# A decoder layer with routed experts on one core: the first normalisation goes to ScalarE, u and k_lo move forward in their lists

## The chip, the cores and the metric

The kernel runs on 1 core of one Trainium2 chip. The metric is the device time of one execution in microseconds, the median of several runs.

## The reference

Input x is 32 sequences of 256 tokens with 256 channels, all float32. Three sublayers follow one another, each with a residual and a layer normalisation:

```python
x = layernorm(x + attn(x))           # a complex decay over the first axis: real(conv) * x
x = layernorm(x + xattn(x, ctx))     # 16 heads of 16 channels, relu projections, softmax, own layernorm
x = layernorm(x + ffn(x))            # rms norm, nearest of 8 centroids picks the expert, a * silu(g)
```

The first sublayer is a recurrence over the 32 items: a complex state per (token, channel) is multiplied by a fixed complex decay and the item is added; the real part (+1 for the residual) times x is what is called u below, and its normalisation over the channels is x1. The cross attention takes queries from x1 and keys and values from the context of the same item.

## The kernel before, in words

There are two phases. Phase 1 makes the first two sublayers and writes each token's row into a bucket of its expert in HBM. Phase 2 runs the experts over tiles of 128 rows; the change does not touch it.

Phase 1 is a software pipeline over the items, unrolled: each engine has its own list, written out by hand, and steps t from -2 to 34 call the same `step(t)` on it. Semaphores alone tie the lists together; an engine never passes an instruction of its own list that waits. In step t the engines work on several items at once: `cur` = t (scores for the maxima), `prv` = t-1 (transposed scores and exponentials), `n` = t+1 (projections), `nn` = t+2 (u and x1), `a` = t-2 (output of the attention and its normalisations), `b` = t-3 (choice of the expert, scatter). Inside a step TensorE, ScalarE and VectorE go through h = 0 to 15; at every even h they do a pair of heads (h, h+1) and, behind it, the other work that the code hangs on that h.

What the change and the prediction speak of:

- TensorE. `scores` (L693) needs the stacks of q and k, which are read from HBM in two halves of 8 heads (`stack_in`), and the maximum of the head two before, because the PSUM banks of the scores are used in turn. `transposed_scores` (L706) needs the exponential of two heads before. The first score matmul of a step is called S0. Then come the flip of x1 (L649 at h = 0, into M_ps[0], which needs `x1_ok` and `ctT_ok`), Q's projection (h = 2, 3), K's projection (L677 at h = 6, 7; it needs the first division of item a, `o_ok`), V's (h = 11, 12).
- VectorE. `maxima` (L888) for a pair of heads takes two instructions. At h = 0 the second normalisation into `row` (L901, waits for `rstd2`). At h = 3 u (L909), one instruction over 128x512 with two inputs in SBUF, `state` and `xt`; at h = 4 its statistics, at h = 5 its moments, between the two parts of `divide`. At h = 11 `slots` and `gain`, at h = 12 y2 (L967, waits for `rstdx`), at h = 13 the two instructions of x1 (L973), which wait for `rstd1` and `y_ok`. L1032 is a small instruction of `pick` with two inputs in SBUF.
- GpSimd. Its list of a step is: `conv_products` (L407, by_re), `weigh` (L465), the bias onto x1 (L495), `cut` for q, `offset`, `conv_real`, `rstd` for ln1, `conv_imag(0)` (L423), `cut` for k (L483, makes k_lo = k32 - k_hi), `conv_imag(1)` (L426), `rstd` for lnx, the two scatters (L513, which wait for the slots from VectorE), `conv_input` (L433, the last of the conv's five counts), `rstd` for ln2 and `rms`.
- ScalarE. Exponentials (L559), the copies of q (L595) and of k (L603: k_hi twice, then k32 twice, by channel half), v_aug (L612) at h = 13, qn at h = 14 and ctT (L580) at h = 15, each behind the pair of that h or of the one before.
- SP, the queue of DMA issues. For item n in order: q pieces out, `read_q` of the first half, k_hi out, wait for `k_cut`, k_lo out (L288), the row of the maxima out (L276), `read_k` of the first half (L301, L302, which waits until both pieces of k are in HBM), and the rest.

Two excerpts, GpSimd's place and the place of x1 on VectorE:

```python
conv_imag(t + 3, 0)
cut(n, k32[:, :, :], k_hi, k_lo, "k_ok", "k_cut", k_out)
conv_imag(t + 3, 1)
```

```python
if h == 13 and active(nn):
    wait(dve, "rstd1", nn, 2)
    wait(dve, "y_ok", nn - 4, 4)
    for c in range(NTC):
        v.tensor_scalar(x1[:, nn.mod(4), c], u[:, c], mv1[:, c, 0:1], rs1[:, 1, c:c + 1],
                        ALU.subtract, ALU.mult).then_inc(s["x1_ok"], 1)
```

Of the kernel before, what the change touches and what calls it, by code (L numbers as in the profile page):

```python
# [10 lines left out]
ALU = mybir.AluOpType  # L11
# [3 lines left out]
P = 128  # L15
# [62 lines left out]
def build(nc, x, ctx_in, lmlg, theta, last_conv, Wq, bq, Wk, bk, Wv, bv, ln_g, ln_b, ffn_scale, centroids, up_w, down_w, out):  # L78
    stack = ExitStack()
    with stack:  # L80
# [33 lines left out]
        def sb1(name, shape, dt=F32):  # L114
            return phase1.enter_context(nc.sbuf_tensor(name, shape, dt))

        with phase1:
# [23 lines left out]
            st1 = sb1("st1", [P, NTC, 6])  # L141
            mv1 = sb1("mv1", [P, NTC, 2])
            rs1 = sb1("rs1", [P, 2, NTC])
            x1 = sb1("x1", [P, 4, NTC, C])
            x1T = sb1("x1T", [P, NCH, TOK])
            ctT = sb1("ctT", [P, NCH, TOK])
# [53 lines left out]
                x_in0 x_in1 ctx_in0 ctx_in1 conv u_ok ln1 rstd1 x1_ok x1T_pe x1T_ok ctT_pe ctT_ok  # L200
                q_pe q_ok k_pe k_ok q_cut k_cut v_pe v_ok q_out0 q_out1 k_out0 k_out1 stack0 stack1 s_pe max_ok
                negT neg_ok neg_out neg_in0 neg_in1 t_pe exp_ok pv o_ev x_pe o_ok qn_pe qn_ok oq_ok lnx rstdx
                x1b_ok y_ok ln2 rstd2 x2_ok rms xw_ok offset nx_ok xnT_pe xnT_ok dist_pe pick rank_pe slot_ok
                id_ok scat0 scat1 pool_waits sp_waits dve_waits"""
            s = {n: sem(n) for n in names.split()}
            x_in, ctx_in_s, q_out, k_out, stack_in = ([s[a + "0"], s[a + "1"]] for a in ("x_in", "ctx_in", "q_out", "k_out", "stack"))
# [161 lines left out]
            def _(pool):  # L368
# [116 lines left out]
                def step(t):  # L485
                    n, a, b = t + 1, t - 2, t - 3
                    first = t.k < 0
                    if first:
                        rstd(t + 2, "ln1", 4, mv1, rs1, "rstd1")
                    conv_products(t + 3)  # L490
                    weigh(b)
                    if active(a):
                        wait(pool, "x1_ok", a, 2)
                        wait(pool, "x1T_pe", a)
                        g.tensor_tensor(x1[:, a.mod(4)], x1[:, a.mod(4)], b_bc[:, :].unsqueeze(1).to_broadcast([P, NTC, C]),  # L495
                                        ALU.add).then_inc(s["x1b_ok"], 1)
                    cut(n, q32[:, :, :], q_hi, q_lo, "q_ok", "q_cut", q_out)
                    offset(b)
                    conv_real(t + 3)
                    if not first:  # L500
                        rstd(t + 2, "ln1", 4, mv1, rs1, "rstd1")
                    conv_imag(t + 3, 0)
                    cut(n, k32[:, :, :], k_hi, k_lo, "k_ok", "k_cut", k_out)
                    conv_imag(t + 3, 1)
                    rstd(a, "lnx", 4, mvx, rsx, "rstdx")
                    if active(b):

                        p = b.mod(2)
                        wait(pool, "slot_ok", b, SLOT)
                        wait(pool, "id_ok", b)  # L510
                        wait(pool, "rms", b, 4)
                        for c in range(NTC):
                            g.indirect_dma_start(out=buckets[:, :], out_offset=bass.IndirectOffsetOnAxis(ap=slot[:, p, c:c + 1], axis=0),  # L513
                                                 in_=row[:, p, c, :], in_offset=None, bounds_check=PAD - 1,
                                                 oob_is_err=False).then_inc(scat[p], 16)
                    conv_input(t + 3)
                    rstd(a, "ln2", 4, mv2, rs2, "rstd2")
                    rms(a)
# [9 lines left out]
            def _(act):  # L528
# [33 lines left out]
                def step(t):  # L562
                    prv, n, a, b = t - 1, t + 1, t - 2, t - 3
                    for h in range(H):
# [44 lines left out]
                        if h == 13 and active(n):  # L609
                            wait(act, "v_pe", n, 2)  # L610
                            wait(act, "pv", n - 4, 4)
                            a_.activation(v_aug[:, n.mod(4), :, 0:H * VW].rearrange("p k (h w) -> p k h w", w=VW)[:, :, :, 0:DH],  # L612
                                          M_ps[1][:, :].rearrange("p (k h w) -> p k h w", k=NTC, w=DH), ACT.Relu).then_inc(s["v_ok"], 1)
                        if h == 4 and active(b):

                            wait(act, "xw_ok", b)
                            wait(act, "rms", b, 4)
                            wait(act, "offset", b - 1)
                            for c in range(NTC):
                                if c:  # L620
                                    wait(act, "nx_ok", b, 2, 1)
                                a_.activation(junk[:, :], xw[:, c], ACT.Square, scale=row[:, b.mod(2), c, C:C + 1],
                                              accum_out=nx[:, c:c + 1]).then_inc(s["nx_ok"], 1)
# [201 lines left out]
            def _(dve):  # L825
# [65 lines left out]
                def step(t):  # L891
                    cur, prv, nn, a, b = t, t - 1, t + 2, t - 2, t - 3
                    for h in range(H):
                        if h % 2 == 0:
                            maxima(cur, h)
                            maxima(cur, h + 1)
                        if h == 0 and active(b):
                            wait(dve, "rstd2", b, 2)
                            wait_ring(dve, scat[b.mod(2)], b - 2, 2, 16 * NTC)
# [1 line left out]
                                v.tensor_scalar(row[:, b.mod(2), c, 0:C], y2[:, c], mv2[:, c, 0:1], rs2[:, 1, c:c + 1],  # L901
                                                ALU.subtract, ALU.mult).then_inc(s["x2_ok"], 1)
                            v.tensor_copy(row[:, b.mod(2), :, C + 1].bitcast(I32), ids[:, b.k]).then_inc(s["id_ok"], 1)
                        if h == 3 and active(nn):

                            wait(dve, "x1_ok", nn - 1, 2)
                            wait(dve, "conv", nn, 5)
                            wait_ring(dve, x_in[nn.mod(2)], nn, 2, 16)
                            v.scalar_tensor_tensor(u[:, :, :], state[:, 0], 1.0, xt[:, nn.mod(2)], ALU.add, ALU.mult).then_inc(s["u_ok"], 1)  # L909
                        if h == 4 and active(nn):  # L910
                            wait(dve, "u_ok", nn)
                            wait(dve, "rstd1", nn - 1, 2)
                            stats(nn, u, st1, "ln1")
                        if h == 5:
                            if active(a):
                                divide(a, 0, 0)
                            if active(nn):
                                moments(nn, st1, mv1, "ln1")
                            if active(a):
                                divide(a, 0, 1)  # L920
                        if h == 6 and active(b):
                            pick(b, 0)
# [20 lines left out]
                        if h == 9 and active(a):  # L943
                            wait(dve, "oq_ok", a, 2)
                            stats(a, oq, stx, "lnx")
                            moments(a, stx, mvx, "lnx")
                        if h == 11:
                            if active(b):
                                slots(b, 0)
# [8 lines left out]
                        if h == 12:  # L958
                            if active(b):
                                slots(b, 3)  # L960
                            if active(a):
# [3 lines left out]
                                for c in range(NTC):  # L965
                                    wait(dve, "y_ok", a, 4, c + 1)
                                    v.scalar_tensor_tensor(y2[:, c], y1[:, c], rsx[:, 1, c:c + 1], x1[:, a.mod(4), c],  # L967
                                                           ALU.mult, ALU.add).then_inc(s["y_ok"], 1)
                        if h == 13 and active(nn):
                            wait(dve, "rstd1", nn, 2)  # L970
                            wait(dve, "y_ok", nn - 4, 4)
                            for c in range(NTC):
                                v.tensor_scalar(x1[:, nn.mod(4), c], u[:, c], mv1[:, c, 0:1], rs1[:, 1, c:c + 1],  # L973
                                                ALU.subtract, ALU.mult).then_inc(s["x1_ok"], 1)
                        if h == 13 and active(a):
                            wait(dve, "y_ok", a, 4)
                            stats(a, y2, st2, "ln2")
# [394 lines left out]
```

## Time and profile before

| | |
|---|---|
| median of 3 runs | 1281.18 us (1277.73 to 1294.08) |
| the profiled execution | 1285.39 us |
| its span in the trace | 1283.3 us |
| busy in the span | TensorE 87%, VectorE 74%, GpSimd 62%, ScalarE 52% |
| mean granted clock of TensorE | 0.935 of full speed |
| phase 1 | up to about 860 us |

The profile is one execution, recorded on the chip. Busy time is the time in which an engine had an instruction under way. Matmuls are pipelined, so a busy TensorE is not one at its peak. A wait is put down to the releaser that came last by the profile.

### The profile page before, as it was taken

How to read it: one execution, taken by the hardware profiler on the slowest of the kernel's cores; microseconds unless marked ns; L12 is line 12 of the kernel's file. 1: busy time of each engine (PE TensorE's matmuls, PEld its weight loads, DVE VectorE, ACT ScalarE, POOL GpSimd, SP SyncE). 2: the span in 40 equal slices, each digit the busy share in tenths (PEclk: the TensorE clock that was granted, in tenths of full speed). 3: DMA queues.
4: the chain of work that ended last, by engine and by line, in shares of the span. 5: the costliest groups of instructions: out<-in, count | busy, mean ns of one | idle time of the engine just before them, and what ended most of it. 6: DMA issues, size and time to landing. Idle time of an engine off the chain costs nothing. (4 is left out here: it accounts for less than half of the span.)

```text
span 1283.3 us, 27523 instructions
## 1 busy us (share of the span) xinstructions
PE 1114.9 (87%) x8060; PEld 817.8 (64%) x8061; DVE 953.8 (74%) x2411; ACT 664.2 (52%) x1413; POOL 792.0 (62%) x943
## 2 busy tenths in 40 slices
PE   0599999999999998999999999830999999999996
PEld 0465666666666666666666666520788888888885
DVE  6357799899899899899899898639455555555553
ACT  1247577676677677776776677514322222222221
POOL 6545778888788888888887865344133333333333
PEclk9859899999899999999999999755999999999998
DMA  5556755655556646656556555206011111111110
GB/s 143 131 158 173 189 144 143 154 138 150 141 142 149 160 130 153 151 146 155 142 146 152 141 134 128 76 25 180 25 53 49 44 52 49 52 46 47 53 49 22
DMA packets 90827, 144.92 MB, mean 113 GB/s; under 512 B 12663, under 2 KB 78336, under 8 KB 84513
## 3 DMA queue, kind: packets, MB, share of 16 engines
q1 hardware_dynamic: 84192, 126.61, 38.3%
q0 software_dynamic: 6528, 16.99, 4.5%
q8 instruction: 55, 0.90, 0.3%
q14 instruction: 52, 0.42, 0.1%
HBM read 91.44 MB, written 53.03 MB: 113 GB/s over the span
## 5 line engine op out<-in xcount | busy, mean ns | idle before, releaser
L888 DVE TENSOR_REDUCE neg_max_sb<-S 128x2 f32<-128x512 f32 x512 | 327.9, 682 | 78.6 <-PE S L693 77.6
L559 ACT ACTIVATE probs<-T 128x512 f32<-128x512 f32 x512 | 278.5, 595 | 152.4 <-PE T L706 140.5
L693 PE MATMUL S<-k_st,q_st 48*128 48x256 f32 x1024 | 215.4, 320 | 51.5 <-DMA k_st<-k_pieces 26.0
L693 PEld LDWEIGHTS S<-k_st,q_st 48*128 48x128 f32 x1024 | 146.7, 193 | 131.1 <-issue 56.3
L706 PE MATMUL T<-q_st,k_st 49*128 49x256 f32 x1024 | 210.5, 318 | 3.7 <-ACT probs L559 2.1
L706 PEld LDWEIGHTS T<-q_st,k_st 49*128 49x128 f32 x1024 | 145.6, 192 | 21.0 <-ACT probs L559 16.2
L1201 ACT ACTIVATE gT<-GT 128x512 f32<-128x512 f32 x71 | 42.6, 600 | 207.5 <-PE GT L1236 207.5
L669 PE MATMUL O<-probs,v_aug 128*32 128x256 f32 x2048 | 147.1, 408 | 0.7 <-ACT probs L559 0.7
L1177 POOL DMA_INDIRECT out<-res,token x71 | 76.4, 1076 | 101.5 <-DVE res L1309 101.5
L1258 PE MATMUL Y<-dn_sb,gT 128*128 x568 | 134.2, 379 | 0.8 <-ACT gT L1201 0.8
L513 POOL DMA_INDIRECT buckets<-row,slot x64 | 66.2, 1034 | 90.4 <-DVE slot L1052 80.2
L1258 PEld LDWEIGHTS Y<-dn_sb,gT 128*128 128x128 f32 x568 | 107.5, 189 | 18.3 <-issue 1.0
L1226 PE MATMUL G<-up_hi,xsT 128*128 x284 | 107.6, 420 | 1.3 <-DVE xsT L1314 1.0
L1182 POOL TENSOR_SCALAR rs<-mv 128x1 f32<-128x1 f32 x71 | 15.9, 224 | 148.7 <-DVE mv L1338 148.6
L1226 PE MATMUL A<-up_hi,xsT 128*128 x284 | 106.8, 417 | 0.0
L1309 DVE TENSOR_SCALAR res<-y,mv,rs 128x256 f32<-128x256 f32 x71 | 29.4, 414 | 85.8 <-POOL rs L1184 85.8
L669 PEld LDWEIGHTS O<-probs,v_aug 128*32 128x32 f32 x2048 | 55.7, 113 | 53.5 <-ACT probs L559 15.0
L407 POOL TENSOR_TENSOR by_re<-state,decay 128x1024 f32<-128x1024 f32 x32 | 75.8, 2368 | 6.0 <-DMA probs<-in_L_ffn_centroids 5.8
L677 PE MATMUL M<-ctT,wk_sb 128*128 128x256 f32 x256 | 67.3, 408 | 6.2 <-issue 6.0
L1205 ACT ACTIVATE gate<-G 128x512 f32<-128x512 f32 x71 | 42.5, 599 | 57.9 <-PE G L1226 57.9
L677 PE MATMUL M<-x1T,wq_sb 128*128 128x256 f32 x256 | 71.2, 426 | 0.7 <-ACT x1T L572 0.7
L796 PE MATMUL M<-wv_sb,ctT 128*128 128x256 f32 x256 | 70.5, 399 | 0.0
(177 smaller groups left out, 2551.6 us busy)
## 6 DMA issues: line engine op xcount, KB each, us to landing
q_st<-q_pieces SPq DMA_DIRECT2D x64, 256.0 KB, 4.7
k_st<-k_pieces SPq DMA_DIRECT2D x64, 256.0 KB, 5.9
xr<-buckets SPq DMA_DIRECT2D x71, 129.0 KB, 2.1
xt<-in_x SPq DMA_DIRECT2D x32, 256.0 KB, 6.4
ct<-in_ctx SPq DMA_DIRECT2D x32, 256.0 KB, 6.8
up_sb<-in_L_ffn_up_w SPq DMA_DIRECT2D x8, 1024.0 KB, 8.6
q_pieces<-q_hi SPq DMA_DIRECT2D x32, 256.0 KB, 2.1
q_pieces<-q_lo SPq DMA_DIRECT2D x32, 256.0 KB, 2.1
```

Of the source, the lines that this page charges most:

```text
L407: g.tensor_tensor(by_re[:, :, :, :], state[:, 0].unsqueeze(1).to_broadcast(both), pair_b, ALU.mult).then_inc(s["conv"], 1)
L513: g.indirect_dma_start(out=buckets[:, :], out_offset=bass.IndirectOffsetOnAxis(ap=slot[:, p, c:c + 1], axis=0), in_=row[:, p, c, :], in_of ...
L559: a_.activation(probs[:, h % 8].rearrange("p k t -> p (k t)"), T_ps[h % 2][:, :], ACT.Exp, scale=DH ** -0.5).then_inc(s["exp_ok"], 1)
L669: last = t_.matmul(O_ps[32 * j:32 * j + 32, (grp % 2) * TOK:(grp % 2 + 1) * TOK], v_aug[:, item.mod(4), kc, h * VW:h * VW + 32], probs[:, ...
L677: last = t_.matmul(dst[:, oc * TOK:(oc + 1) * TOK], w[:, ic, oc * P:(oc + 1) * P], xT[:, ic, :], start=(ic == 0), stop=(ic == NCH - 1))
L693: last = t_.matmul(S_ps[h % 2][:, c * TOK:(c + 1) * TOK], q_st[base:base + STACK, h, c * P:(c + 1) * P], k_st[base:base + STACK, h, :], st ...
L706: last = t_.matmul(T_ps[h % 2][:, c * TOK:(c + 1) * TOK], k_st[base:base + AUG, h, c * P:(c + 1) * P], q_st[base:base + AUG, h, :], start= ...
L796: last = t_.matmul(M_ps[1][:, c * C:(c + 1) * C], ctT[:, ic, c * P:(c + 1) * P], wv_sb[:, ic, :], start=False, stop=(c == NTC - 1 and ic = ...
L888: v.tensor_reduce(neg_max[:, cur.mod(2), :, h], S_ps[h % 2][:, :].rearrange("p (c t) -> p c t", c=NTC), AX.X, ALU.max, negate=True).then_i ...
L1177: g.indirect_dma_start(out=out_rows, out_offset=bass.IndirectOffsetOnAxis(ap=token[:, f.mod(2):f.mod(2) + 1], axis=0), in_=res[:, f.mod(2) ...
L1226: last = t_.matmul(ps[:, :], xT[:, w, c * P:(c + 1) * P], src[:, bass.ds(off + c * 2 * HID, HID)], start=(k == 0), stop=(k == len(terms) - 1))
L1258: last = t_.matmul(Y_ps[:, 0:C], gT[:, m.mod(2), c * P:(c + 1) * P], dn_sb[:, bass.ds(off + c * C, C)], start=(c == 0), stop=(c == HCH - 1))
```

## The change

Three edits, all in phase 1.

1. The two instructions of x1 leave VectorE. ScalarE does them at h = 13, behind v_aug and ahead of the exponentials of heads 14 and 15, as Identity with a scale (1/std) and a bias. The bias is -mean/std, `shift`, a new instruction of VectorE at h = 10 on 128x2 elements.
2. u moves from h = 3 to h = 0, right behind maxima 0 and 1 and ahead of `row`. Its statistics and moments follow together at h = 2.
3. On GpSimd `cut` for k moves ahead of `conv_imag(0)`.

```diff
@@ GpSimd
+                    cut(n, k32[:, :, :], k_hi, k_lo, "k_ok", "k_cut", k_out)
                     conv_imag(t + 3, 0)
-                    cut(n, k32[:, :, :], k_hi, k_lo, "k_ok", "k_cut", k_out)
                     conv_imag(t + 3, 1)
@@ ScalarE
+                        if h == 13 and active(n + 1):
+                            nn = n + 1
+                            wait(act, "shift", nn)
+                            wait(act, "y_ok", nn - 4, 4)
+                            for c in range(NTC):
+                                a_.activation(x1[:, nn.mod(4), c], u[:, c], ACT.Identity, bias=shift[:, c:c + 1],
+                                              scale=rs1[:, 1, c:c + 1]).then_inc(s["x1_ok"], 1)
@@ VectorE
+                        if h == 0 and active(nn):
+                            wait(dve, "x1_ok", nn - 1, 2)
+                            wait(dve, "conv", nn, 5)
+                            wait_ring(dve, x_in[nn.mod(2)], nn, 2, 16)
+                            v.scalar_tensor_tensor(u[:, :, :], state[:, 0], 1.0, xt[:, nn.mod(2)], ALU.add, ALU.mult).then_inc(s["u_ok"], 1)
...
-                        if h == 3 and active(nn):
...
-                        if h == 4 and active(nn):
+                        if h == 2 and active(nn):
                             wait(dve, "u_ok", nn)
                             wait(dve, "rstd1", nn - 1, 2)
                             stats(nn, u, st1, "ln1")
+                            moments(nn, st1, mv1, "ln1")
                         if h == 5:
                             if active(a):
                                 divide(a, 0, 0)
-                            if active(nn):
-                                moments(nn, st1, mv1, "ln1")
-                            if active(a):
                                 divide(a, 0, 1)
...
+                        if h == 10 and active(nn):
+                            wait(dve, "rstd1", nn, 2)
+                            v.scalar_tensor_tensor(shift[:, :], mv1[:, :, 0], -1.0, rs1[:, 1], ALU.mult, ALU.mult).then_inc(s["shift"], 1)
...
-                        if h == 13 and active(nn):
-                            wait(dve, "rstd1", nn, 2)
-                            wait(dve, "y_ok", nn - 4, 4)
-                            for c in range(NTC):
-                                v.tensor_scalar(x1[:, nn.mod(4), c], u[:, c], mv1[:, c, 0:1], rs1[:, 1, c:c + 1],
-                                                ALU.subtract, ALU.mult).then_inc(s["x1_ok"], 1)
```

## Rows read from the trace of the kernel before

**Rows 1.** Windows: busy us (instructions) of PE, PEld, DVE, ACT, POOL; clock, DMA share, GB/s
```profile
510.00:610.00 100.00, 91.79 (x822) 62.99 (x822) 91.45 (x235) 70.89 (x156) 84.08 (x93) 0.98 0.60 152
```

**Rows 2.** Waits from 110 to 810 us: total us, times, longest
```profile
POOL buckets L513 <- DVE slot L1052: 67.1, 28, 3.3
...
PEld S L693 <- DMA k_st<-k_pieces: 32.6, 22, 2.3
```

**Rows 3.** TensorE in order of time: start us, us, instruction [idle before <-releaser]
```profile
130.23 1.11 PE L649 MATMUL M<-ident,x 128*128 128x128 f32 x4
...
489.58 0.35 PE L693 MATMUL S<-k_st,q_st 48*128 48x256 f32 x1 [0.83 <-DVE neg_max_sb L888]
...
495.36 0.38 PE L693 MATMUL S<-k_st,q_st 48*128 48x256 f32 x1
...
499.54 1.97 PE L677 MATMUL M<-ctT,wk_sb 128*128 128x256 f32 x8 [0.67 <-issue]
...
513.48 0.50 PE L693 MATMUL S<-k_st,q_st 48*128 48x256 f32 x2 [1.79 <-DMA k_st<-k_pieces]
...
537.38 0.35 PE L693 MATMUL S<-k_st,q_st 48*128 48x256 f32 x1 [0.72 <-DVE neg_max_sb L888]
...
751.65 0.66 PE L649 MATMUL M<-ident,x 128*128 128x128 f32 x4
```

**Rows 4.** The DMA issues of SP in order of time
```profile
505.86 0.38 SPq L288 DMA_DIRECT2D k_pieces<-k_lo  x1
...
509.08 0.32 SPq L301 DMA_DIRECT2D k_st<-k_pieces  x1
...
530.87 0.38 SPq L288 DMA_DIRECT2D k_pieces<-k_lo  x1
...
533.03 0.32 SPq L301 DMA_DIRECT2D k_st<-k_pieces  x1
```

**Rows 5.** GpSimd in order of time
```profile
493.68 2.37 POOL L407 TENSOR_TENSOR by_re<-state,decay 128x1024 f32<-128x1024 f32 x1
...
502.82 1.26 POOL L423 TENSOR_TENSOR state<-state,decay 128x512 f32<-128x512 f32 x1
504.05 1.79 POOL L483 TENSOR_TENSOR k_lo<-k,k_hi 128x512 fp32r<-128x512 f32 x1
...
507.59 0.96 POOL L442 TENSOR_TENSOR rsx<-rsx,neg_half 128x2 f32<-128x2 f32 x1
...
537.55 1.29 POOL L433 TENSOR_TENSOR state<-state,xt 128x512 f32<-128x512 f32 x1
```

**Rows 6.** VectorE in order of time
```profile
492.07 0.74 DVE L901 TENSOR_SCALAR row<-oq,mv,rs 128x256 f32<-128x256 f32 x2 [0.70 <-POOL rs L442]
...
494.07 2.52 DVE L909 SCALAR_TENSOR_TENSOR u<-state,xt 128x512 f32<-128x512 f32 x1
...
504.51 0.16 DVE L1032 TENSOR_TENSOR onehot_bf<-expert_no,choice 128x16 bf16<-128x16 f32 x1
...
509.24 0.88 DVE L967 SCALAR_TENSOR_TENSOR oq<-o,rsx,x 128x256 f32<-128x256 f32 x2
510.23 0.74 DVE L973 TENSOR_SCALAR x<-u,mv,rs 128x256 f32<-128x256 f32 x2
...
511.54 1.27 DVE L888 TENSOR_REDUCE neg_max_sb<-S 128x2 f32<-128x512 f32 x2
```

**Rows 7.** ScalarE in order of time
```profile
502.28 0.84 ACT L603 ACTIVATE k<-M,bk_sb 128x256 f32<-128x256 f32 x2
...
510.50 1.09 ACT L559 ACTIVATE probs<-T 128x512 f32<-128x512 f32 x2 [0.87 <-PE T L706]
...
511.95 0.62 ACT L580 ACTIVATE ctT<-M 128x512 f32<-128x512 f32 x1
```

**Rows 8.** Groups: one line's ns min/median/max; others' busy us, mean ns | idle before
```profile
L909 DVE SCALAR_TENSOR_TENSOR u<-state,xt x32: 682/2023/2527, 27.4 to 755.2; 128x512 f32<-128x512 f32 x32
...
L1032 DVE TENSOR_TENSOR onehot_bf<-expert_no,choice 128x16 bf16<-128x16 f32 x29 | 16.9, 582 | 0.0
```

More of the change, by code:

```diff
@@ L143, in build @@
             rs1 = sb1("rs1", [P, 2, NTC])
+            shift = sb1("shift", [P, NTC])
             x1 = sb1("x1", [P, 4, NTC, C])
@@ L202, in build @@
                 negT neg_ok neg_out neg_in0 neg_in1 t_pe exp_ok pv o_ev x_pe o_ok qn_pe qn_ok oq_ok lnx rstdx
-                x1b_ok y_ok ln2 rstd2 x2_ok rms xw_ok offset nx_ok xnT_pe xnT_ok dist_pe pick rank_pe slot_ok
+                x1b_ok y_ok ln2 rstd2 x2_ok rms xw_ok offset shift nx_ok xnT_pe xnT_ok dist_pe pick rank_pe slot_ok
                 id_ok scat0 scat1 pool_waits sp_waits dve_waits"""
@@ L903, in step @@
                             v.tensor_copy(row[:, b.mod(2), :, C + 1].bitcast(I32), ids[:, b.k]).then_inc(s["id_ok"], 1)
-                        if h == 3 and active(nn):
[L906 to L909, printed above, removed]
-                        if h == 4 and active(nn):
+                        if h == 2 and active(nn):
                             wait(dve, "u_ok", nn)
```

## Prediction

> **What bounds the kernel now.** I looked at the stages first (the table by windows), then at the waits, then at one turn of the pipeline on each engine. The first phase fills about 860 of the 1283 us, and its middle is a steady pipeline: in a typical stretch TensorE is busy 91.79 of 100 us and VectorE 91.45, GpSimd 84.08, ScalarE 70.89, at a granted clock of 0.98 [rows 1]. Two engines near 92% do not say which one sets the pace, so the waits are read next. TensorE's weight loads waited for the k stack's DMA 22 times, 32.6 us together, in 29 steps; GpSimd waited 28 times for VectorE's slots, 67.1 us [rows 2]. The rest of phase 1 and the whole of phase 2 are not touched by the change.
>
> TensorE's flips of x1 (L649, one in each step) at 130.23 and 751.65 have 25 others between them: 26 steps of (751.65 - 130.23)/26 = 23.90 us [rows 3]. The same period is seen from the first score matmul, S0: 489.58, 513.48 and 537.38, twice 23.90 [rows 3]. Now follow k through the step that starts at 489.58. K's projection starts at 499.54 and takes 1.97 [rows 3]; ScalarE's last copy of k ends at 502.28 + 0.84 = 503.12 [rows 7]; GpSimd is in conv_imag(0) until 502.82 + 1.26 = 504.08, then makes k_lo, 504.05 + 1.79 = 505.84 [rows 5]; its write is issued at 505.86, the read of the stack at 509.08 [rows 4], and S0 of the next step, which waited 1.79 us for it, starts at 513.48 [rows 3]. That is a closed loop: write to read 3.22 us here and 2.16 in the next step (530.87 to 533.03), read to S0 4.40 and 4.35 us [rows 3, 4]. This loop is the first bound. The second is right behind it: at 537.38 S0 is put down to the maxima (0.72 us) [rows 3], and in the step of 489.58 the maximum of head 14 ended at about 511.54 + 0.68 = 512.22, half of the pair's row [rows 6], so VectorE would have allowed a period of 22.64.
>
> **The change part by part**, in us after S0 of a step, S0 = 489.58 being 0.
>
> *k_lo ahead of conv_imag(0).* GpSimd reaches that place at 502.82 - 489.58 = 13.24, the copies of k are there at 13.54. So today 0.96 of the 14.47 at which k_lo starts is the conv instruction. Nothing is added to GpSimd but perhaps a wait for k, and behind it stand conv_imag, 1/std of "lnx" (ends 507.59 + 0.96 = 508.55 [rows 5], or 18.97) and the scatter, which waits for its slot anyway, 67.1/28 = 2.4 us a step [rows 2]. y2 on VectorE starts at 509.24 [rows 6], 0.7 after that 1/std, so 0.7 of delay is covered.
>
> *u right behind maxima 0 and 1.* u takes 0.68 alone, 2.02 in the median, 2.53 at most [rows 8]. The row of 494.07 shows why: it lasted until 496.59, 0.54 after the end of GpSimd's by_re (493.68 + 2.37 = 496.05) [rows 5, 6]: it was held until that instruction was done. In the new place by_re is not running yet, and I price u at 0.70: 1.8 us less in a step like this one, 1.3 less than the median. Against that: u needs conv_input, which ends at 537.55 + 1.29 = 538.84, 1.46 after S0 [rows 3, 5], and maxima 0 and 1 end at 1.8. In the new kernel VectorE's end of a step is shorter, so the slots, the scatter and conv_input stand later against S0, I estimate by 0.6: conv_input ends at 2.1, u waits 0.35 for it and ends at 2.85, GpSimd's two instructions for 1/std of "ln2" end at 3.55, and L901, which waits for them today too (0.70 us), starts at 3.65 instead of 492.07 - 489.58 = 2.49 [rows 6]. Maxima 2 and 3 end at 5.65 instead of 4.5 (u starts right behind them today, at 494.07). TensorE wants them for head 4, whose first matmul starts at 495.36, 5.78 after S0 [rows 3]: just covered. Then statistics and moments come at once, by an estimate from L973 (0.74) and L1032 (0.16 each) about 1.1 together with the latency between them that nothing hides now. Maxima 4 and 5 and the first division are done at 8.7 instead of 9.86, and K's projection, which stood idle 0.67 before 499.54 [rows 3], starts at 9.3 instead of 9.96. The copies of k end near 12.9 to 13.2.
>
> The Trainium skill has the rule for it: in "SBUF — State Buffer", section "Who interferes with whom", a VectorE instruction with two SBUF inputs and a GpSimd instruction that reads SBUF exclude each other for the whole instruction. The row of u agrees. By that rule the new two-input "shift" instruction would be held as well, which speaks against the change; the sum takes its price from a row, next.
>
> *First normalisation on ScalarE.* VectorE loses L973, two instructions in 0.74 us [rows 6], and gains "shift", on 128x2 elements. Not shown in the trace. Its floor is 0.16, L1032 when nothing held it; its ceiling is 1.4, that and a whole GpSimd instruction of the conv (1.26) [rows 5, 6]. The nearest row is the small two-input L1032, 0.58 in the mean [rows 8]: I take 0.58, so the trade is worth only 0.15. ScalarE gains two instructions, by the two copies of k, of the same size and with a bias too, 0.84 for the pair [rows 7]. They stand behind v_aug and ahead of the exponentials of heads 14 and 15, and they wait for y2: 509.24 + 0.88 = 510.12 now [rows 6]. Queued behind them: exponentials 14 and 15 (start 510.50 now, 1.09), qn and ctT (ends 511.95 + 0.62 = 512.57) [rows 7], and on ctT waits TensorE's flip of x1 in the next step. ScalarE's idle share is large, but not at this spot.
>
> *Summing the loops.* (1) k: GpSimd arrives at 13.24 + 0.6 = 13.8, later than k's copies; k_lo takes 1.5 (1.26 alone as L423, 1.79 when held) and ends at 15.3 instead of 16.26; + 2.16 to 3.22 + 4.4 gives 21.9 to 22.9, middle 22.4. (2) VectorE: 1.15 ahead at the first division, most of it lost at maxima 6 and 7, since S6 itself is not earlier; 0.4 ahead at maxima 8 to 11, 0.2 behind after shift, 0.44 ahead at the maximum of head 14: 22.64 - 0.44 = 22.2. (3) ScalarE: y2 starts 0.2 later than today's 19.66 and ends at 20.8; + 0.1, x1 0.84, exponentials 1.09, qn and ctT 1.1 = 23.9, where the flip would like to start at 22.4 + 0.95 = 23.35. Its delay of up to 0.5 is not all passed on. Three bounds so near together are worth more than the largest of them: I take 22.9. Gain 23.90 - 22.90 = 1.0 a step, 26 steps: 26 us. The steps ahead of 130 us and behind 751 I leave at nothing.
>
> The profiled execution took 1285.4 (span 1283.3 and 2.1 around it): 1285.4 - 26 = 1259.4. It is 4.2 above the median of the three runs, 1281.2, so against the median I forecast 1255. About 2% (25.6 us, a time of 1255.6) is what a measurement of this kernel tells from no change, and the forecast lies on that border.
>
> **The rivals.**
>
> *A: another chain takes over, gain small.* If shift costs its ceiling (0.8 more), VectorE's turn is 23.0, and with the ScalarE tail passed on in full (0.5) the period is 23.4: 0.5 x 26 = 13, 1268. For it: VectorE is at 91% and its two-input instructions are held now. Against: u alone gives back more than shift can take.
>
> *B: the stalls vanish altogether.* TensorE's own work, from S0 489.58 to where it falls idle at 511.69 (513.48 - 1.79), is 22.11, of it 0.67 idle before K [rows 3]: with 22.0 a step the gain is 1.9 x 26 = 49, 1232. For it: the k loop's lower end is 21.9. Against: (2) and (3) would both have to have slack.
>
> *C: slower, through the new link from GpSimd to ScalarE.* Now GpSimd waits for k with conv_imag behind it, so k's copies → k_lo → both conv_imag → 1/std → y2 → x1 on ScalarE → exponentials → ctT → flip is one chain, with x1 new in it. From the end of k's copies to the flip: 0.05 + 1.79 + 2.52 + 1.5 + 0.1 + 0.88 + 0.1 + 0.84 + 1.09 + 1.1 = 9.9. It decides if the copies end later than 23.9 + 0.9 - 9.9 = 14.9 after S0; today 13.54. What could bring it there is TensorE's lower clock level at the start of a step, as after a stall: the four transposes of the flip took 1.11 us at 130.23 and 0.66 at 751.65 [rows 3]. If the first 3.5 us of each step ran so, that is 3.5 x (1.11/0.66 - 1) = 2.4 us, the copies end at 15.9 and the period is 24.9: 1.0 x 26 = 26 more, 1307. For it: nothing hides the tail of ScalarE, and each stall can bring the next. Against: 1.4 us of room, and K's projection comes earlier, not later.
>
> *D: no effect*, since the k stack's DMA comes no earlier: the write or the read is late for another reason (write of the maxima's row ahead of the read in SP's queue). 1281. Against: today that write goes out 0.5 after k_lo's without waiting. I count it with A's upper end.
>
> **How the numbers follow.** Forecast (period 22.6 to 23.2, 1247 to 1263) 0.48; A with D (1263 to 1285) 0.27; B (below 1247) 0.17; C 0.08. Half of the forecast's case lies beyond 2%, so faster by over 2% is 0.24 + 0.17 = 0.41; within 2% 0.24 + 0.27 = 0.51; slower 0.08. The range for 8 in 10 goes from 1234 (most of B is above it) to 1281 (A without the worst of D). It holds the bounds of shift's price, of k_lo's and of the DMA's.
>
> **What would show it.** Right: x1's flips 22.9 apart; u at about 0.7 us, one instruction ahead of L901; k_lo's start less than 0.3 behind the end of k's copies or right behind 1/std; waits for the k stack below 32.6 us; L973 gone from VectorE and an Identity row of about 0.84 for the pair on ScalarE; shift between 0.15 and 1.3 in its mean. The row "probs L559 <- PE T" on ScalarE shrinks, and a wait of TensorE's flip for ctT appears. Wrong: periods near 23.9 with the k wait unchanged (D), u's mean above 1.5 because the conv chain is late, a large new wait of x1 on ScalarE for y2 (A or C), or TensorE's granted clock well under 0.98 in the stretch 510 to 610.

## The result, and the profile after

The changed kernel takes 1294.99 us in the median (1288.12 to 1307.88, 20 runs), the kernel before 1285.64 (1277.11 to 1295.16, 20 runs): a ratio of 1.007 (1.0041 to 1.0098). It is 0.7% slower, where 1255 had been forecast. The range started at 1234 and ended at 1281, so the result lies outside it. One of the 20 runs of the changed kernel, and one of the four of `after_conv` below, was slow, over 1.5% above the fastest of its kernel; the medians include them, the ratios do not. The profiled execution took 1290.80, with a span of 1288.7.

A stretch of the table by windows of the changed kernel, the columns as in [rows 1]:

```profile
510.00:610.00 100.00, 90.32 (x800) 62.83 (x798) 86.37 (x229) 73.38 (x162) 82.06 (x91) 1.00 0.58 143
```

In these 100 us VectorE is busy 5 us less than before, GpSimd 2 less, TensorE 1.5 less, only ScalarE 2.5 more, and it is far from full; TensorE's granted clock is 1.00 here. The three busy engines are less busy, and the kernel is slower. So none of them is the bound by its work alone: something passes from one to the other. The waits from 110 to 810 us:

```profile
ACT probs L560 <- PE T L714: 90.5, 63, 3.2
POOL buckets L514 <- DVE slot L1055: 86.0, 28, 3.3
DVE neg_max_sb L896 <- PE S L701: 56.1, 71, 2.6
...
ACT x L620 <- DVE oq L976: 29.9, 28, 1.4
PEld M L783 <- DVE onehot_bf L1035: 22.3, 22, 1.1
...
PE M L657 <- ACT ctT L581: 14.3, 26, 0.6
...
PEld S L701 <- DMA k_st<-k_pieces: 10.3, 11, 1.8
```

Against [rows 2] the wait for the k stack fell from 32.6 to 10.3 us, as intended. GpSimd's wait for the slots grew from 67.1 to 86.0. TensorE's weight loads wait for onehot_bf, a small table from `pick` that says which expert each token chose, 22 times and 22.3 us; before it was 11 times and 6.5 us. The groups of VectorE and ScalarE that the forecast priced (busy us, mean ns), and onehot_bf, called onehot from here on:

```profile
L1035 DVE TENSOR_TENSOR onehot_bf<-expert_no,choice 128x16 bf16<-128x16 f32 x28 | 28.8, 1029 | 0.0
L910 DVE SCALAR_TENSOR_TENSOR u<-state,xt 128x512 f32<-128x512 f32 x27 | 18.7, 691 | 10.5 <-issue 10.4
L955 DVE SCALAR_TENSOR_TENSOR shift<-mv,rs 128x2 f32<-128x2 f32 x28 | 4.8, 173 | 0.0
L620 ACT ACTIVATE x<-u,shift,rs 128x256 f32<-128x256 f32 x56 | 30.6, 593 | 29.9 <-DVE oq L976 29.9
```

u fell to 0.69 and shift costs 0.17. But onehot_bf, an instruction that the change does not touch, went from 582 ns [rows 8] to 1029. The trace in order of time shows how. GpSimd:

```profile
486.89 1.08 POOL L514 DMA_INDIRECT buckets<-row,slot  x1 [3.22 <-DVE slot L1055]
...
502.38 1.28 POOL L484 TENSOR_TENSOR k_lo<-k,k_hi 128x512 fp32r<-128x512 f32 x1
503.62 1.69 POOL L424 TENSOR_TENSOR state<-state,decay 128x512 f32<-128x512 f32 x1
...
510.83 1.08 POOL L514 DMA_INDIRECT buckets<-row,slot  x1 [3.21 <-DVE slot L1055]
```

VectorE in the same step:

```profile
490.65 0.69 DVE L910 SCALAR_TENSOR_TENSOR u<-state,xt 128x512 f32<-128x512 f32 x1 [0.48 <-issue]
...
502.82 1.34 DVE L1000 TENSOR_TENSOR oq<-o,qn 128x256 f32<-128x256 f32 x1
504.07 1.26 DVE L1035 TENSOR_TENSOR onehot_bf<-expert_no,choice 128x16 bf16<-128x16 f32 x1
505.26 0.74 DVE L880 BATCH_NORM_STATS2 stx<-oq 128x6 f32<-128x256 f32 x2
...
509.86 0.16 DVE L1055 CAST slot<-slot_f 128x2 uint32<-128x2 f32 x1
```

oq starts while k_lo runs and ends 0.5 behind it (503.66 to 504.16). conv_imag(0), which had been standing behind oq since 503.62, goes next, until 505.31, and onehot, which was next on VectorE, ends with it (505.33). This is what I call the hold. It is seen in the same way in all 171 held steps of the ten kernels that have onehot at this place: onehot ends 0.02 to 0.04 us behind the GpSimd instruction that was standing.

From there VectorE works without a gap, but for 0.16 behind its statistics, until the slots (510.02), on which GpSimd's scatter waits (510.83). And GpSimd works from its scatter at 486.89 to 505.31 without a gap but the 0.30 between the scatters and less than 0.1 between small instructions. That closes a loop, from one scatter to the next: 18.42 on GpSimd, 4.71 on VectorE, 0.81 from the slots to the scatter, together 23.94. The sum must be the distance of the two scatters; what counts is that no stretch of it has slack. TensorE, with the first score matmul S0, the flip and K's projection:

```profile
488.38 0.47 PE L701 MATMUL S<-k_st,q_st 48*128 48x256 f32 x2 [0.44 <-DVE neg_max_sb L896]
...
490.12 0.63 PE L657 MATMUL M<-ident,x 128*128 128x128 f32 x4 [0.56 <-ACT ctT L581]
...
498.37 2.00 PE L685 MATMUL M<-ctT,wk_sb 128*128 128x256 f32 x8
...
514.07 0.63 PE L657 MATMUL M<-ident,x 128*128 128x128 f32 x4 [0.56 <-ACT ctT L581]
```

The flips are 23.95 apart, and 17 of the 26 periods are between 23.92 and 23.97. Before, the periods were scattered from 22.6 to 26.2. The mean of the 26 is 24.08 instead of 23.90 [rows 3]; 26 times that difference is 4.7 of the 5.4 us by which the two profiled executions differ, while the medians differ by 9.35, so this pair of profiles shows about half of the loss. Onehot was not held in four steps. One of them ran at a granted clock of 1.00 (onehot at 457.03, 0.20 us) and took 22.74, near the period that I had forecast; the other three ran at 0.90 to 0.93 and took 24.24 to 25.07. In every kernel here the steps below 1.00 are the longer ones: in the changed kernel 24.70 in the mean of seven, against 23.85 in the 19 at 1.00 (23.53 in the 17 of the kernel before). Whether a long step lowers the clock or the clock lengthens the step, these means do not say.

The time to k's read, SP's queue in the same step:

```profile
503.69 0.38 SPq L289 DMA_DIRECT2D k_pieces<-k_lo  x1
...
506.93 0.32 SPq L302 DMA_DIRECT2D k_st<-k_pieces  x1
```

k_lo's write is issued 13.91 after the flip in the mean of the 26 steps instead of 15.56, but from write to read it now takes 3.53 instead of 2.47. Part of the 1.65 is the flip itself, which now starts 1.66 after S0 instead of 1.05. Counted from S0 the write is 1.03 earlier and the read is not earlier at all, 19.11 against 19.08.

### The profile page after: what moved, and what is told of

Its sections match the earlier page's. It is cut to its first block and busy times, and to the rows that moved or that the text cites. A ratio compares the mean times of both kernels' runs of the same rounds, so it can differ in the third digit from the quotient of the medians.

```text
span 1288.7 us, 27555 instructions
## 1 busy us (share of the span) xinstructions
PE 1114.7 (87%) x8060; PEld 821.6 (64%) x8061; DVE 920.6 (71%) x2379; ACT 691.1 (54%) x1477; POOL 784.2 (61%) x943
## 5 line engine op out<-in xcount | busy, mean ns | idle before, releaser
L714 PE MATMUL T<-q_st,k_st 49*128 49x256 f32 x1024 | 214.3, 320 | 2.7 <-ACT probs L560 1.8
L685 PE MATMUL M<-x1T,wq_sb 128*128 128x256 f32 x256 | 68.6, 414 | 0.7 <-ACT x1T L573 0.7
```

Of the source, the lines that this page charges most:

```text
L685: last = t_.matmul(dst[:, oc * TOK:(oc + 1) * TOK], w[:, ic, oc * P:(oc + 1) * P], xT[:, ic, :], start=(ic == 0), stop=(ic == NCH - 1))
L714: last = t_.matmul(T_ps[h % 2][:, c * TOK:(c + 1) * TOK], k_st[base:base + AUG, h, c * P:(c + 1) * P], q_st[base:base + AUG, h, :], start= ...
```

## The experiments

All ratios are against the kernel before, with 95% intervals; 18 kernels ran. "Period" is the mean between the flips of 26 steps, the ones of [rows 3]; "held" counts the steps of 26 in which onehot took over 0.8 us (11 before, 22 after). Both come from one profiled execution of each kernel, so small differences between periods mean little; the ratio is the measure.

| run | edit | median us | ratio | period | held |
|---|---|---|---|---|---|
| late_onehot | changed kernel, onehot behind the moments | 1276.9 | 0.9936 (0.9898 to 0.9974) | 23.52 | 1 |
| late_x1 | changed, x1 behind exponentials 14, 15 | 1290.7 | 1.0056 (1.0025 to 1.0087) | 24.33 | 18 |
| onehot_scalar | changed, onehot with one SBUF input | 1294.7 | 1.0079 (1.0046 to 1.0112) | 24.28 | all |
| u_x1 | changed, edit 3 undone | 1289.8 | 1.0043 (1.0009 to 1.0077) | 23.92 | 17 |
| k_u | changed, edit 1 undone | 1297.9 | 1.0133 (1.0068 to 1.0198) | 24.15 | 21 |
| k_x1 | changed, edit 2 undone | 1296.6 | 1.0119 (1.0079 to 1.0158) | 24.06 | 13 |
| k_only | before, edit 3 alone | 1287.6 | 1.0026 (0.9995 to 1.0058) | 23.81 | 10 |
| before_onehot | before, onehot behind the moments | 1279.8 | 0.9951 (0.9909 to 0.9994) | 23.74 | 1 |
| after_qread | changed, q's read behind k_lo's write | 1286.8 | 1.0026 (0.9993 to 1.0059) | 23.89 | 20 |
| onehot_qread | late_onehot and after_qread | 1260.8 | 0.9846 (0.9797 to 0.9894) | 23.05 | 1 |
| after_conv | changed, conv_input ahead of the scatters | 1305.9 | 1.0159 (1.0101 to 1.0218) | 24.94 | 13 |
| all_three | onehot_qread and conv_input | 1258.1 | 0.9794 (0.9753 to 0.9835) | 22.89 | 1 |
| before_three | before with the three moves | 1317.8 | 1.0272 (1.0228 to 1.0317) | 24.98 | 2 |
| u_x1_onehot | late_onehot, edit 3 undone | 1280.0 | 0.9973 (0.9942 to 1.0005) | 23.93 | 1 |
| good_no_k | onehot_qread, edit 3 undone | 1318.1 | 1.029 (1.0221 to 1.036) | 24.88 | 1 |
| good_no_x1 | onehot_qread, edit 1 undone | 1263.8 | 0.9853 (0.9782 to 0.9925) | 23.16 | 2 |
| good_no_u | onehot_qread, edit 2 undone | 1269.1 | 0.9894 (0.9861 to 0.9926) | 23.24 | 1 |
| three_no_x1 | all_three, edit 1 undone | 1272.7 | 0.9906 (0.9876 to 0.9936) | 23.08 | 2 |

**Is it the hold of onehot, or ScalarE's tail?** My rival C had named the tail: x1 on ScalarE, the exponentials, ctT, the flip. "Port theory" in the expectations is the other reading: conv_imag(0) on GpSimd keeps the two-input onehot on VectorE waiting. late_onehot:

```diff
-                            if active(b):
-                                pick(b, 5)
                         if h == 9 and active(a):
...
                             moments(a, stx, mvx, "lnx")
+                        if h == 9 and active(b):
+                            pick(b, 5)
```

> The changed kernel with onehot_bf (two inputs in SBUF) moved behind the statistics and moments of lnx on VectorE. Port theory: in 22 of 26 steps onehot is held 1.26 us by conv_imag(0), and the loop VectorE - slots - scatter - conv - onehot sets the period of 23.95; with the statistics ahead of it the 0.74 to 1.1 us are used, onehot is short (0.2), the period falls to 22.8 to 23.2 and the time is about 1262 to 1275, ratio to the kernel before 0.98 to 0.99. Tail theory (x1 on ScalarE, ctT and the flip set the period): no change, 1290 to 1297.

late_x1 moves the block of x1 on ScalarE from h == 13 to h == 14, behind the exponentials of the pair (14, 15).

> The changed kernel with x1 on ScalarE behind the exponentials of heads 14 and 15 instead of ahead of them. Tail theory: the exponentials start about 1 us earlier, TensorE's T of head 0 and 1 too, and the period falls by 0.3 to 0.5, 1282 to 1288. Port theory: TensorE and ScalarE have slack against the loop of VectorE and GpSimd, the period stays 23.95 and the time 1290 to 1297, with onehot held in 20 or more of 26 steps.

The first gave 1276.9, 1.3% less than the changed kernel (0.9936 against 1.007), a little above the 1262 to 1275 that I expected of the port theory; the second gave 1290.7, within the interval of the changed kernel, though with 18 held steps where I had expected 20 or more. VectorE in late_onehot, and conv_imag(0) of the same step:

```profile
472.39 1.34 DVE L1000 TENSOR_TENSOR oq<-o,qn 128x256 f32<-128x256 f32 x1
473.77 0.75 DVE L880 BATCH_NORM_STATS2 stx<-oq 128x6 f32<-128x256 f32 x2
474.68 0.25 DVE L886 BATCH_NORM_AGGREGATE mvx<-stx 128x2 f32<-128x6 f32 x2 [0.16 <-DVE stx L880]
474.84 0.14 DVE L1035 TENSOR_TENSOR onehot_bf<-expert_no,choice 128x16 bf16<-128x16 f32 x1
```

```profile
473.19 1.70 POOL L424 TENSOR_TENSOR state<-state,decay 128x512 f32<-128x512 f32 x1
```

The statistics and the moments now run beside conv_imag(0), and onehot takes 0.14. 12 of the 26 periods are 22.96 to 23.12 and one is 22.71, all at a granted clock of 1.00; the others are 23.16 and more, and eight of them ran below 1.00. TensorE's weight loads still wait for the k stack 15 times, 12.0 us. So the hold is shown to be worth about 1 us in a step that nothing else disturbs (23.95 to 22.97), and 0.57 in the mean of the 26.

The second test is weaker than I took it for. In late_x1 x1 stands behind the exponentials, but still ahead of qn and ctT, and the flip still starts 1.5 after S0. It shows only that the exponentials do not decide. The test of the whole tail is k_u below, where x1 is not on ScalarE: the flip starts 1.01 after S0, no wait of it for ctT is listed, and the kernel is no faster (1.0133, period 24.15). With the hold in place the tail is not the bound.

**Is it the second SBUF input?** In onehot_scalar the instruction stands at its own place:

```diff
-                        v.tensor_tensor(onehot_bf[:, :, :], expert_no[:, :, :], ch, ALU.is_equal).then_inc(s["pick"], 1)
+                        for c in range(NTC):
+                            last = v.tensor_scalar(onehot_bf[:, c], expert_no[:, c], choice[:, c:c + 1], None, ALU.is_equal)
+                        last.then_inc(s["pick"], 1)
```

> The changed kernel with onehot_bf at its own place, written as two instructions (one for each half of the tokens) with one input in SBUF and choice as the scalar, instead of one with two inputs. Port theory: with one input it isn't held by conv_imag(0): 0.2 to 0.3 us for the two instead of 1.09, and the period falls from 23.95 to 22.9 to 23.2 in most steps, as in late_onehot: 1268 to 1282. If it was not the second input that held it (any instruction of VectorE there waits, or the statistics' new place was what helped in late_onehot): held as before, 1288 to 1298.

It took 1294.7, as slow as the changed kernel. The row of its two instructions:

```profile
503.59 1.39 DVE L1036 TENSOR_SCALAR onehot_bf<-expert_no,choice 128x8 bf16<-128x8 f32 x2
```

A tensor_scalar with one tensor in SBUF and a scalar from SBUF is held as well, now in every step. So my port theory in its narrow form (only two inputs are held) is wrong: this form is held too, while the statistics (L880), put at the same place in late_onehot, take 0.75 for the two beside conv_imag(0), as they did elsewhere. The Trainium skill, in "SBUF — State Buffer", section "Who interferes with whom", lists tensor_scalar among the VectorE instructions that can take the shared pair when their operands meet its conditions. This row agrees with it, 1.39 us for the two.

**The k stack's DMA.** k_only is the third edit by itself.

> The kernel before with the third edit alone: k_lo ahead of conv_imag(0). If the k loop was the bound, as I forecast, the k stack is read 0.9 us earlier and the period falls by 0.5 to 0.9: 1260 to 1272. Port theory: the wait for the k stack nearly goes, but VectorE with x1 and the long u is the bound and its onehot may be held more often: 1278 to 1292, period 23.6 to 24.2.

It gave no gain (1.0026, interval around 1), though k_lo's write went out 1.5 us earlier (14.08 behind the flip, 15.56 before): write to read grew from 2.47 to 3.40 and read to S0 from 4.82 to 5.34. after_qread and onehot_qread move q's read:

```diff
-                    read_q(nxt, 0)
...
                     write_piece(nxt, k_dram, 1, k_lo, k_out)
+                    read_q(nxt, 0)
```

> late_onehot with the read of the first half of q's stack moved in SP's queue from ahead of k_hi's write to behind k_lo's write. DMA theory: in the changed kernel k_lo is written 1.65 us earlier but the time from its write to the read of the k stack grew from 2.47 to 3.5 in the mean, since its write stands behind that 256 KB read; with the read out of the way it falls to 2.2 to 2.7, the stalls for k with their steps of 24.2 go, and the period falls from 23.5 to 23.0: 1260 to 1270, ratio 0.982 to 0.99. Rival (the DMA engines are shared, order only shifts the delay): write to read falls, but read to S0 grows from 4.6 to 5.3 or more, and the time stays at 1272 to 1280.

> The changed kernel with q's read behind k_lo's write alone. Loop theory: the period is set by VectorE and GpSimd at 23.95, so an earlier k stack saves only the steps that stall for it: 1284 to 1294, period 23.9 to 24.0. If the k stack's DMA is the bound, as forecast: 1262 to 1278.

With the hold in place q's read gives little (1.0026 against 1.007, period 23.89). With the hold gone it gives nearly 1% more: 0.9846 against 0.9936, write to read 2.79 instead of 3.46 (2.72 instead of 3.53 in after_qread), and 19 of the 26 periods are 23.0. Read to S0 grew from 4.76 to 5.11, which does not decide whether the transfers delay each other, since S0 also waits for VectorE. So about 0.7 to 0.8 us of the earlier k_lo had been given back behind q's 256 KB read. That the rest was hidden by the loop is argued, not shown by itself.

**The loop, shortened another way.** after_conv moves one line of GpSimd:

```diff
+                    conv_input(t + 3)
                     if active(b):
                         p = b.mod(2)
                         wait(pool, "slot_ok", b, SLOT)
...
-                    conv_input(t + 3)
```

> The changed kernel with conv_input moved ahead of the two scatters in GpSimd's list, so that it is done while GpSimd waits for the slots (3.2 us in the step of 510.83). Loop theory: slots - scatter - conv_input - the rest of GpSimd's list up to the instruction that holds onehot - VectorE back to the slots is a closed loop without idle time of 23.95 us; 1.28 us less in it gives 22.7, up to what the k stack and onehot's hold allow: period 22.8 to 23.5, 1258 to 1276. If the loop is not that one: 1290 to 1297, with only u's wait of 0.47 gone.

It was a clear miss: 1305.9. Its profile is of the longest of its runs, 1318.88 us, at a mean clock of 0.915, so I read only its steps at a granted clock of 1.00. VectorE and GpSimd in one of 24.66 us:

```profile
464.89 1.28 DVE L1035 TENSOR_TENSOR onehot_bf<-expert_no,choice 128x16 bf16<-128x16 f32 x1
...
468.48 1.51 DVE L1007 SCALAR_TENSOR_TENSOR o<-oq,mvx,g_bc 128x256 f32<-128x256 f32 x1
```

```profile
468.44 1.27 POOL L434 TENSOR_TENSOR state<-state,xt 128x512 f32<-128x512 f32 x1
```

conv_input now starts just ahead of the gain (L1007, 0.48 at most in the 26 steps of the changed kernel), and holds it for 1.0 us, ahead of the slots. That happens in the 13 steps in which onehot is held too. Of the eight steps at a clock of 1.00, six have both holds and take 24.66 to 24.68; two have neither and take 22.74 and 22.77. So in these steps the loop, shortened by 1.27, was lengthened again by a hold. The other 18 ran at 0.87 to 0.98, with a mean of 25.27; why the clock was lower there is open. all_three:

> The changed kernel with onehot behind the moments, q's read behind k_lo's write and conv_input ahead of the scatters. Loop theory: onehot_qread's period was locked at 22.97, again by the loop through GpSimd, 1.28 shorter now; TensorE and ScalarE's tail are next: 21.9 to 22.5, 1232 to 1252, ratio 0.965 to 0.978. Rival (TensorE's flip, which waits for ctT behind x1 on ScalarE, or VectorE alone is the bound at 22.9): 1257 to 1264.

0.9794 (0.9753 to 0.9835), with 21 periods of 22.7: the fastest of all kernels. It beats onehot_qread by less than the intervals, and it stands at the time of the rival in the expectation, not at mine: the loop is 1.27 shorter, and the undisturbed period fell only from 22.97 to 22.66. What sets 22.7 there was not isolated.

**What each edit is worth.** On the changed kernel, with the hold:

> The changed kernel without its third edit: conv_imag(0) again ahead of k_lo. Port theory: the hold of oq and onehot depends on where GpSimd's list stands; with k_lo behind, onehot meets k_lo as in the kernel before and may be held less often, but the k stack comes 1.2 us later, so the k loop sets the period: 23.2 to 23.8, 1270 to 1285. Tail theory: as the changed kernel or slower, 1290 to 1300.

> The changed kernel with x1 back on VectorE (no shift): edits 2 and 3 only. Port theory: VectorE has 0.74 - 0.17 = 0.57 us a step more in the loop with GpSimd, in front of the slots or behind them: L973 stands behind the slots, so it is not in that loop, and the period stays near 23.95 with onehot held in most steps: 1288 to 1298. Tail theory: without x1 ahead of the exponentials the period falls to 23.0 to 23.5: 1262 to 1278.

> The changed kernel with u back at h = 3: edits 1 and 3 only. Port theory: the long u (2.0 to 2.5) comes back, but VectorE is then later at oq and onehot, so the meeting with GpSimd's instructions changes: onehot held in about half the steps, period 23.4 to 24.0, 1272 to 1290. If u's move was worth its 1.3 us and the rest neutral: 1300 or more.

Undoing the third edit gives 1.0043, the first 1.0133, the second 1.0119, against 1.007 for the changed kernel; all three intervals overlap that of the changed kernel. The first expectation for k_u, a period near 23.95 without x1 on ScalarE, fits (24.15, many steps 24.0). For u_x1 and k_x1, as for before_onehot and good_no_u below, the times lie between the two ranges that I had written down and decide between them only in part. So the third edit helps nothing here: without it onehot is held less often (17 of 26), while the weight loads wait for the k stack 30.3 us instead of 10.3. Once the hold is cured:

> onehot_qread with k_lo behind conv_imag(0) again, so edits 1 and 2 with the hold of onehot cured and q's read moved. By the forecast the third edit is worth about 1 us a step: period 23.5 to 24.0, 1275 to 1290. If it is worth nothing there (conv_imag(0) and k_lo are the same length, and GpSimd holds VectorE as long either way): 1257 to 1266.

> onehot_qread with x1 on VectorE again, so edits 2 and 3. By the forecast's prices VectorE loses 0.74 - 0.15 = 0.6 us a step if it is the bound at the end of a step: period 23.3 to 23.7, 1268 to 1280. If the loop through the slots is all that counts (x1 stands behind them): period 22.97, 1257 to 1264.

> onehot_qread with u at h = 3 again, so edits 1 and 3. u is held by by_re then, 1.3 us more on VectorE in the middle of the loop: period 23.5 to 24.3, 1272 to 1295. If the first half of a step has slack on VectorE, as its waits for S there say: period 22.97 to 23.2, 1257 to 1266.

> late_onehot with k_lo behind conv_imag(0) again and q's read at its own place: edits 1 and 2 with onehot's hold cured. good_no_k also had q's read behind k_lo's late write, which delays q's own stack; here that is left out. If the third edit is worth what reached the read of the k stack in the changed kernel (k_lo's write 1.65 earlier, 1.06 given back behind q's read): 0.6 us a step slower than late_onehot, about 1287 to 1297. If good_no_k's loss was q's read alone: the same as late_onehot, 1272 to 1281.

u's move is worth 0.5% (0.9894 against 0.9846), at intervals that overlap, x1's nothing that can be told (0.9853). For k_lo the fair pair is late_onehot and u_x1_onehot: 0.9936 against 0.9973, 0.4% at intervals that overlap. good_no_k, 1.029, missed both of its ranges and is another thing: k_lo is written 15.78 behind the flip there, q's read stands behind it at 16.25 instead of 11.70 in u_x1_onehot, read to S0 is 5.18 instead of 4.44, and the weight loads waited 49.9 us for the k stack at a mean clock of 0.914. So k_lo ahead is what makes q's later place pay. before_three shows the same (q's read at 16.40, 43.2 us of waits for the k stack), and I had expected 1255 to 1275 of it:

> The kernel before with the same three moves (onehot, q's read, conv_input) and none of the change's edits. It says whether the change pays once the loop is cut: by the forecast's terms (u 1.3, x1 0.57, k_lo 1.2) it should be slower than all_three by 0.5 to 1.0 us a step, 1255 to 1275. If the change gives nothing even then: the same as all_three within 5 us.

> The kernel before with onehot behind the statistics and moments of lnx. In the kernel before onehot was held in 11 of 26 steps. If VectorE's loop is the bound there too, its period falls by 0.3 to 0.5: 1270 to 1277. If the k loop is (the forecast's first bound), nothing moves but the hold: 1281 to 1288, period 23.7 to 24.0.

> all_three with x1 back on VectorE: edits 2 and 3 with the three moves. good_no_x1 was not slower than onehot_qread. If x1's move is worth nothing, as there: 1250 to 1262. If VectorE is the bound once the loop is cut by conv_input: 0.6 a step slower, 1268 to 1278. Port theory adds a risk: L973 or the gain may then meet conv_input and be held 1.0 us more, 1275 to 1300.

before_onehot gained 0.5%, so the kernel before also paid for the hold in its 11 steps. That bears on what the change is worth: with onehot's move in both, the kernel before stands at 0.9951 (0.9909 to 0.9994) and the changed one at 0.9936 (0.9898 to 0.9974), no difference that can be told. The hold explains why the change lost; its cure alone does not bring the gain that was forecast. That came only with q's read moved too.

three_no_x1 took 1272.7, in the range of its second expectation. 17 of its periods are 22.5 or 22.6, below the 22.7 of all_three, but six are 23.6 or more, and its ratio is 1.1% higher than that of all_three. So x1 on ScalarE does not make the undisturbed step shorter there. That it makes the pipeline steadier is my reading of one profile, and good_no_x1 does not show it.

## Why the prediction was wrong

- *k_lo ahead, term (1).* Right on GpSimd: its end was forecast at 15.3 after S0 and was at 503.66 - 488.38 = 15.28. Wrong behind it: I took write to read from two rows, 2.16 and 3.22, and it became 3.53 in the mean, behind q's read; and read to S0, taken as 4.4, was 4.97 in the mean, in part because VectorE was late. The forecast had looked at the row of the maxima in SP's queue, not at q's read ahead of the write.
- *u.* Right: 0.69 against 0.70; its wait for conv_input 0.48 against 0.35; L901 at 3.58 after S0 against 3.65. But K's projection started at 9.99, not at 9.3: the flip waits for ctT and starts 1.74 after S0 instead of 0.94, and from there TensorE has no gap to K's projection.
- *First normalisation.* shift was never held in the 26 steps (0.17 in the mean, 0.32 at most, against 0.58). x1 on ScalarE cost 1.09 for the pair against 0.84.
- *The sum, term (2), is the step that failed.* "0.4 ahead at maxima 8 to 11" took the durations of oq and onehot from the old meeting with GpSimd. In the new order oq meets k_lo and onehot meets conv_imag(0): 0.98 and 1.03 in the mean instead of 0.92 and 0.58. In the mean of the 26 steps the maximum of head 8 ended 0.35 later after S0 than before, that of head 10 0.95 later, that of head 14 0.33 later (23.82 against 23.49), where 0.44 ahead was forecast. In late_onehot head 10 is level with before (17.67 against 17.63) and head 14 ends at 23.04, 0.45 ahead. I had cited the very rule, and applied it to the new instruction only, not to the old ones that stand beside the moved ones.
- *How much each was worth.* From the forecast 22.9 to the measured 24.08 there are 1.18 us a step. Onehot's move gives back 0.57 (to 23.52), q's read another 0.47 (to 23.05).
- *Three bounds, each by itself.* I had moved conv_input back by 0.6 against S0 as a consequence, without seeing that slots, scatter, conv and VectorE form a closed loop without slack. By the rows of the changed kernel that loop is 23.94. With onehot's hold out of it the undisturbed period is 22.97. That this is close to the forecast 22.9 is luck: the 22.9 was a guess above bounds of 22.4, 22.2 and 23.35, and the loop was not among them.
- *Rivals.* A came nearest (another chain takes over), but it named shift's hold, which did not come, and the tail, which k_u rules out, and ended at 1268. C had "slower" right, but its mechanism, x1 in ScalarE's tail, is real (a 0.56 wait at most flips) and did not decide. D was false: the k wait fell to a third.
- *The signs.* Nearly all that I had listed as showing me right came true: u's price, k_lo's place, the shorter k wait, shift, the smaller "probs <- PE T" (131.4 to 90.5 us). Only the period did not. Each sign watched a part that was moved, none an instruction beside it. The one sign of A or C, x1 waiting for y2 on ScalarE, was there (29.9 us, 28 times). C's sum of the chain is also 0.1 short: its terms add up to 10.0, not 9.9.

## What to carry to other kernels

When an instruction of one engine is moved, list what the other engine does at its new and its old time, and reprice every instruction there that can be held, however small: 128x16 elements cost a whole microsecond in 22 of 26 steps. Look for closed loops through two queues: follow the stretches without a gap from an instruction to the same one a step later. In the changed kernel a period that was the same to 0.05 us in 17 of 26 steps was the sign of such a loop. And undo or mend one thing at a time on top of the changed kernel: the change lost 0.7%, and with two pieces moved beside it the kernel gained 1.5%. Make each such move on the kernel before as well: late_onehot, 0.6% faster than the kernel before, looks like a gain by the change, until before_onehot shows 0.5% without it. The kernel before with both moves, onehot's and q's read, and nothing else was not run; good_no_k and before_three, both slow with q's read behind a late k_lo, suggest that it would lose.

## What the runs showed of the hardware

Where a GpSimd instruction was standing behind oq on VectorE, onehot, the next on VectorE, lost to it in 22 of 26 steps of the changed kernel as a tensor_tensor, and in all 26 as two tensor_scalar; in the kernel before it lost in 11 of 26. In these two kernels it was all or nothing: 0.15 to 0.20 us or 1.25 to 1.28; at its later place, in late_onehot, one of 26 took 1.05 and the others 0.14. Each held onehot ended 0.02 to 0.04 us behind the GpSimd instruction. What decides which of the two goes first was not found.

An Identity of ScalarE with a scale and a bias from SBUF, its input in SBUF too, took 593 ns for 128x256; the copy of k, from PSUM and with a bias alone, took 480. Which of the two differences costs the time was not tested.

An earlier write did not arrive earlier in proportion: in k_only it was issued 1.5 us earlier behind the flip, and the read that waits for it 0.55 us earlier (17.48 instead of 18.03).
